# Layer 0's transposition behind the aggregation, its projection at the head of the next step

## The reference

```python
# layer 0
e_of = lambda a: leaky(einsum('bid,bjd->bij', h * a[:, 0], h))
alpha = where(adj == 1, e0, neg_inf)        # the drawn adj holds only 0 and 1
x = layernorm(x + einsum('bij,bjd->bid', sigmoid(alpha), h) + bias)
# layer 1
Hh = einsum('bni,io->bno', h, W)            # the projection
s, d = Hh @ a_src, Hh @ a_dst
e = where(adj != 0, exp(-leaky_relu(s[:, :, None] + d[:, None, :])), 0)
x = layernorm(x + elu(einsum('bnm,bmo->bno', e, Hh) / rowsum))
```

## Time and profile before

| | |
|---|---|
| median of 3 runs | 1391.45 us (1388.99 to 1396.03) |
| the profiled execution | 1394.09 us |
| its span, first to last instruction | 1392.4 us |
| mean granted TensorE clock | 0.982 |
| PE busy | 1288.6 us (93%) |
| weight loads (PEld) busy | 1153.7 us (83%) |
| DVE busy | 1020.3 us (73%) |
| ACT busy | 858.3 us (62%) |
| POOL busy | 837.5 us (60%) |

### The profile page before, as it was taken

One profiled execution on the slowest core, in us unless ns is written; L12 is line 12 of the kernel. 1 busy time (PEld: TensorE's weight loads), 2 busy tenths in 40 slices (PEclk: granted clock), 3 DMA queues, 4 the chain that ended last, 5 costly groups with the idle time before them and its releaser, 6 DMA issues.

```text
span 1392.4 us, 27439 instructions
## 1 busy us (share of the span) xinstructions
PE 1288.6 (93%) x7874; PEld 1153.7 (83%) x7874; DVE 1020.3 (73%) x2594; ACT 858.3 (62%) x2129; POOL 837.5 (60%) x1228
## 2 busy tenths in 40 slices
PE   4898999999999999999999999999999999999996
PEld 3787888888888898888888888898888988888885
DVE  3776777777787777777777787777777777787765
ACT  3664757567584765757557584765747667584742
POOL 4554848467394755838477394755838467394732
PEclk9999999999999999999999999999999999999998
DMA  5537162351706327162441706326162351706201
GB/s 128 73 53 119 23 103 68 60 113 30 130 29 99 82 32 137 26 98 68 67 110 27 134 24 102 79 34 136 26 98 68 63 111 30 132 27 93 57 1 33
DMA packets 190352, 101.73 MB, mean 73 GB/s; under 512 B 140656, under 2 KB 173808, under 8 KB 190320
## 3 DMA queue, kind: packets, MB, share of 16 engines
q1 hardware_dynamic: 171888, 67.79, 22.3%
q0 software_dynamic: 18432, 33.56, 16.4%
HBM read 84.55 MB, written 16.78 MB: 73 GB/s over the span
## 4 chain that ended last, share of the span: by engine, by line
PE 44%; POOL 23%; DVE 18%; issue 7%; ACT 6%; DMA 1%; DVEq 1%; POOLq 0%; SPq 0%; ACTq 0%
POOL coef_lo L367 12%; PE acc_bank L1210 11%; PE hh_bank L1189 6%; PE acc_bank L1091 5%; DVE coef L868 5%; PE acc_bank L1092 5%; PE acc_bank L1093 5%; PE lg_bank L1091 3%; PE lg_bank L1093 3%; PE lg_bank L1092 3%; POOL rstd L388 3%; DVE reluP L902 2%; POOL rstd L378 2%; DVE stats L910 2%; DVE resid L905 2%
## 5 line engine op out<-in xcount | busy, mean ns | idle before, releaser
L1210 PE MATMUL acc_bank<-H,coef 128*128 128x258 f32 x2048 | 470.0, 383 | 19.5 <-ACT reluP L606 18.2
L1210 PEld LDWEIGHTS acc_bank<-H,coef 128*128 128x128 f32 x2048 | 382.2, 190 | 82.8 <-issue 28.9
L367 POOL TENSOR_TENSOR coef_lo<-coef,coef_hi 128x1024 fp32r<-128x1024 f32 x128 | 305.7, 2389 | 58.4 <-ACT coef_hi L554 57.7
L1091 PE MATMUL acc_bank<-h_hi,coef_hi 128*128 128x256 f32 x1024 | 303.4, 296 | 1.8 <-issue 1.8
L1092 PE MATMUL acc_bank<-h_lo,coef_hi 128*128 128x256 f32 x1024 | 292.2, 285 | 0.0
L1093 PE MATMUL acc_bank<-h_hi,coef_lo 128*128 128x256 f32 x1024 | 292.0, 285 | 0.0
L868 DVE SCALAR_TENSOR_TENSOR coef<-tr_bank,E_col,codeT 128x256 f32<-128x256 f32 x512 | 209.2, 476 | 38.2 <-PE acc_bank L1210 35.7
L353 POOL DMA_DIRECT2D code_nat<-in_adj x128 | 73.5, 575 | 229.5 <-DMA codeT<-code_nat 209.1
L1091 PEld LDWEIGHTS acc_bank<-h_hi,coef_hi 128*128 128x128 f32 x1024 | 199.9, 195 | 2.8 <-issue 2.0
L1092 PEld LDWEIGHTS acc_bank<-h_lo,coef_hi 128*128 128x128 f32 x1024 | 200.2, 196 | 0.0
L1093 PEld LDWEIGHTS acc_bank<-h_hi,coef_lo 128*128 128x128 f32 x1024 | 199.9, 195 | 0.0
(11 more groups left out here) (76 smaller groups left out, 2295.4 us busy)
## 6 DMA issues: line engine op xcount, KB each, us to landing
code_nat<-in_adj POOLq DMA_DIRECT2D x128, 256.0 KB, 3.7
x_raw<-in_x SPq DMA_DIRECT2D x16, 1024.0 KB, 5.6
out<-x SPq DMA_DIRECT2D x128, 128.0 KB, 1.7
codeT<-code_nat SPq DMA_TRANSPOSE x128, 3.6
W_ext<-in_L_gnn_W SPq DMA_DIRECT2D x1, 256.0 KB, 2.9
score<-in_L_gnn_a SPq DMA_DIRECT2D x1, 256.0 KB, 6.7
bias_bc<-in_L_gnn_bias SPq DMA_DIRECT2D x1, 128.0 KB, 4.0
a_col<-in_L_gnn_a SPq DMA_DIRECT2D x4, 1.0 KB, 2.2
```

The lines of the kernel that those rows point to most:

```text
L367: nc.gpsimd.tensor_tensor(coef_lo[:, t % 4, :, :], blocks(coef[:, t % 4, :]), f32(coef_hi[:, t % 4, :, :]), ALU.subtract).then_inc(S.lo0, 1)
L1091: nc.tensor.matmul(dst, lhs_hi, rhs_hi, start=first, stop=False)
L1210: ins = nc.tensor.matmul(acc_bank[t % 2][:, 0:HC], coef[:, SLOT1[t], J * P:(J + 1) * P], H[:, J, :], start=J == 0, stop=J == NT - 1)
```

## The change

On PE, tr(t-2) moves behind agg(t) in every step from 2 on, and proj(t-3) opens step t, ahead of mirror and agg(t). proj(5) stands behind step 7. The spreads of g are gathered: four behind tr(4) in step 6, and number 4 stands with number 5 after the scores' chunks 2 and 3. On ACT, `keep_x1T(t-2)` moves from the second place of step t to its end, for t = 2 to 7. Nothing is added or taken away.

```diff
@@ ACT
-                    if t >= 2:
-                        keep_x1T(F, b, t - 2, prev)
+                    if t == NT:
+                        keep_x1T(F, b, 6, prev)
...
                     if t in (6, 7):
                         watch_codes(b, t)
+                    if 2 <= t < NT:
+                        keep_x1T(F, b, t - 2, prev)
@@ PE
                 for t in range(NT):
                     if t >= 3:
-
-                        pe.wait_ge(F.x1T_kept, NT * b + t - 2)
-                        transpose_x1(F, b, t - 2)
+                        project(F, b, t - 3, prev)
                     if 1 <= t and t + 3 < NT:
                         mirror(b, t + 3)
                     aggregate0(F, b, t, prev)
-                    if t == 2:
-                        if prev:
-
-                            pe.wait_ge(F.x1T_kept, NT * b)
-                        transpose_x1(F, b, 0)
-                    if t >= 3:
-                        project(F, b, t - 2, prev)
-                    if t == 5:
-                        for u in range(3):
+                    if t >= 2:
+
+                        if t >= 3 or prev:
+                            pe.wait_ge(F.x1T_kept, NT * b + t - 2)
+                        transpose_x1(F, b, t - 2)
+                    if t == 6:
+                        for u in range(4):
                             spread_G(b, u)
-                    if t >= 6:
-                        spread_G(b, t - 3)
...
-                    if t == 2:
-                        project(F, b, 0, prev)
-
+                project(F, b, 5, prev)
                 pe.wait_ge(F.x1T_kept, NT * b + 6)
                 transpose_x1(F, b, 6)
                 if nxt:
                     scores_chunk(b + 1, 2)
                     scores_chunk(b + 1, 3)
+                spread_G(b, 4)
                 spread_G(b, 5)
```

## The result

The changed kernel takes 1451.0 us (median of 4 runs, 1449.4 to 1451.4) against 1391.5 before: ratio 1.0418, 95% interval 1.0398 to 1.0437. It is slower by about 4%, 59.5 us by the medians. The profiled execution took 1450.7 us with a span of 1448.9, 56.5 us longer than before; the mean granted clock is 0.973 instead of 0.982. No instruction was added, so all of it is waiting and clock.

What follows compares the result with a forecast made beforehand. PE was taken to bound the kernel. 1394.1 us profiled, +46.5 for 15 graphs at 3.1, +7 clock, +5 last graph made 1452.6; less the profiled execution's 2.6 above the median, forecast 1450 us, range 1418 to 1462.

Steps and rivals of the forecast that it cites:

- The wait changes places, and grows: Step 2: the wait at tr(1) goes, proj(0) waits instead; agg(3) starts 0.8 us later, idle stretch 1.96 + 1.14 us.
- The round: Steps 3 and 4: PE and ACT wait for each other in turn, 5.47 us per round, ACT setting the pace.
- Steps 5 to 7: proj(3) to proj(5) follow PE's work and the way through ACT; chunk 2 starts 3.0 us later, 3.1 with spread 4.
- Nothing comes back behind chunk 2: Behind the scores' chunk 2 the order is as before and PE dense, so the 3.1 us per graph stay lost.
- The clock: Low clock after the longer idle stretch, 1.0 us in three graphs of four: 11 less 4 already paid, +7 us.
- The last graph: Without high_xT and scores ACT's round hides, but the bare way through ACT in steps 3 to 7 costs: +5 us.
- The sum: 1394.1 + 46.5 + 7 + 5 = 1452.6 us for the profiled execution; forecast 1450 us.
- The wait only changes places: Rival, 10%: the round of steps 3 and 4 is shorter than added up; +29 us, 1420 us.
- POOL and DVE set the pace anyway: Rival, 3%: PE is ahead of them at tr(3), so a PE later by under 0.65 us costs nothing; 1390 us.
- faster: Rival, 3%: keep_x1T is through before PE wants it, and the wait at tr goes; 1349 us.
- Signs foretold: PE's wait at tr under 5 us, proj's some 85 us, graph period about 87 us, windows 0.94 in most graphs.

Runs made afterwards that it cites:

- short check: Changed kernel, and kernel before, with the check of the codes on ACT over 128 columns instead of 1024: 1438.1 us and 1389.6 us.
- filled kernels: Extra products that nothing reads in PE's idle stretch: five ahead of proj(0) in the changed kernel, 1433.5 us; four ahead of tr(1) in the kernel before, 1384.7 us.

## Why the prediction was right

- **The wait changes places, and grows.** Forecast: proj(0) at 404.87 in the time of the graph before, hence 416.81 with the shift; measured 416.86. The cause is as given, the copy behind `high0(5)` and the mask of tile 5: ACT shows 0.26 us of waiting for DVE ahead of it.
- **The round.** Forecast 5.47 us; measured 422.37 - 416.86 = 5.51 and again 5.51. The short check and the filled kernels show the round as the bound: a term shortened inside it comes out, and a changed clock leaves it as it is. Its reach was smaller than the forecast had it. From proj(1) to proj(2) the changed kernel takes 5.5 us in every graph but the last, but from proj(0) to proj(1) only in three; in the twelve with a fall of the clock it takes 6.3 to 7.6, and in nine of these proj(1) comes without any wait: the stretched agg(3) holds PE, not ACT's copy. The forecast had 6.1 for such a graph.
- **Steps 5 to 7.** Forecast proj(3) 432.58, proj(4) 437.66, proj(5) 442.38, chunk 2 443.49; measured 432.54, 437.71, 442.18, 443.29. The small miss is step 7, priced at 0.2 us too much. The loss per graph at chunk 2 is thus 2.8 us and not 3.0, the loss by spread 4 not counted.
- **Nothing comes back behind chunk 2.** From proj(0) at 939.18 to proj(0) at 1025.26, two rows at the full clock, are 86.1 us; before, tr(1) to tr(1) took 83.1. 3.0 us in a whole graph, with 3.1 forecast. (Not every period is alike: from 416.86 to 503.31 it is 86.4.)
- **The clock** was the term with the widest bounds, and it was sized too small. I took 11 falls of 1.0 us. There were 12 in the 15 graphs with a next one, and two sorts of them. From proj(0) to proj(5) the graph at the full clock takes 442.18 - 416.86 = 25.3 us; those at 0.94 take 0.8 to 0.95 us more, those at 0.88 about 2.0 more. Together this is 13.7 us, where I had 11. The last graph, for which I had counted none, adds 2.3: from proj(0) to proj(5) it takes 25.6, and 23.2 in the filled kernel. Both together are near the 17.6 that the fill wins. In the kernel before the fill wins 5 to 7, where I had counted 4 to 5.
- **The last graph.** From tr(0) to its last spread it took 1348.99 - 1318.54 = 30.5 us before, and 1404.00 - 1367.99 = 36.0 now: 5.5, forecast 5. This agreement is luck. In the two filled kernels, where the clock doesn't fall there, the same stretch takes 30.4 and 33.7. So the order costs 3.3, where I had 5, and the rest is the clock.
- **The sum.** The traces of the filled kernels take it apart. From proj(0) of graph 1 to proj(0) of the last graph, 14 periods, it is 1167.6 us before and 1217.1 changed, and 1163.6 and 1202.8 with the fills. Filled against filled the order costs 39.2 us, or 2.8 per graph, where I had 14 x 3.1 = 43.4. The clock costs 1217.1 - 1202.8 = 14.3 in the changed kernel and 1167.6 - 1163.6 = 4.0 before: 10.3 more, where I had 7 in all. (The other 7.0 of the 56.5 us lie ahead of graph 1 and behind the last proj(0).) So the order was priced some 4 us too high and the clock some 4 too low, and the agreement to a microsecond (forecast 1452.6 for the profiled execution, measured 1450.7) is luck; the two mechanisms are not. This split is good to a few us only, since the profiled execution of the changed, filled kernel lies 4.9 us under its median.
- **The rivals.** The wait only changes places fails at the 5.5 us between the projections; POOL and DVE set the pace anyway fails at the 86.1 us period; faster fails since the copy ends at 416.44 + 0.37 - 11.94 = 404.87 in the time of the graph before, not by 404.1. The change on PE that was to bring the gain does bring it, 1% alone, but not with ACT's half.
- **Signs foretold.** The wait of tr goes to 0 (forecast under 5), that of proj to 80.1 (forecast 85). The mean period is 1217.1 / 14 = 86.9 us (forecast about 87). The wait at proj(5) is 0.47 us, not 0.8, and proj(1) hardly waits in the graphs with a fall; longer waits at proj(0), 3.3 to 3.45 us, make up for most of it.
- The strict order of PE's products, which I took from the Trainium skill (TensorE: Matmul & The Clock Gate, Part 2), shows again here: in the 3.28 us ahead of proj(0) PE's timeline holds no product of agg(3), though its last operand, `coef_lo` of tile 3, was ready at 409.66.
- By the Trainium skill's warning of idle gaps (the same page, the table on why this matters for kernels) the low clock would come in each graph. The trace agrees for 13 of 16: two graphs have 3.28 and 3.45 us of idle time and 1.00 in their windows, and the first has a shorter wait.

## What to carry to other kernels

- When an item moves on one engine, write down everything that then stands ahead of it and what each of these waits for. Here a 0.4 us copy came to stand behind an instruction that waits for a third engine, and PE's whole list stood behind the copy.
- Two engines that hand work to and fro in fixed orders form a round. Add up the round from starts in a gapless stretch; if it is longer than the work of either, it sets the pace. Before a wait is priced, look for what is ready next: here a wait that was taken away came back in full one step later.
- Test the halves of a two-sided reordering apart: here one half was worth -1% and the other +3.3%, and the pair (+4.2%) hid a gain.

## What the runs showed of the hardware

- Useless products in an idle stretch pay. 2.3 us of them in each graph took 17.6 us off the changed kernel, and 1.8 us of them 5 to 7 us off the kernel before. In both filled traces the granted clock stays at 1.00 over layer 0's part from graph 1 on.
- The same wait had three outcomes. After idle stretches of 3.43 to 3.45 us the granted clock over the 28 us is 0.94 in some graphs, 0.88 in others and 1.00 in one. At 1.2 GHz instead of 2.4, 0.88 is twice as much time at the low level as 0.94, and it costs 2.0 us where 0.94 costs 0.8 to 0.95. What decides between them the runs don't show. In the kernel before it is the same with stalls of 1.96 to 2.16 us, of which eight were followed by the low level and the others not.
